# Sorted rows carry their token's number, POOL scatters each tile's results to token order, and batch 0's norm and half its scans move beside tiles

## What is computed

```
expert, layer 0:  silu(x @ wg.T) * (x @ wu.T) @ wd.T           # per token, for its top 2 of 8
scan, layer 1:    s = exp(dt * A) * s + (dt * x) * b           # over 1024 tokens, 16 states a channel
                  y = sum over the states of s * c
expert, layer 1:  square(relu(x @ w_fc.T)) @ w_proj.T          # top 2 of 8, and one shared expert
out:              weight_1 * first choice + weight_2 * second choice + residual, then a norm
```

## Time and profile before

| | |
|---|---|
| median of 3 runs | 1080.74 us (1079.37 to 1081.22) |
| profiled execution | 1075.24 us |
| its span, first to last instruction | 1073.5 us |
| granted TensorE clock, mean | 0.925 of 2.4 GHz |
| busy | PE 913.9, DVE 728.1, ACT 770.0, POOL 501.1 us |
| indirect DMAs | 64 scatters to `xs`, 64 gathers from `ys` |
| stores of tiles by SP | 92 |

### The profile page before, as it was taken

The page is one execution under the profiler, slowest core; times in us unless marked ns, Lnnn a source line. Parts: engine busy times, 40 slices in busy tenths (PEclk is TensorE's granted clock), DMA queues, the critical chain, the costliest instruction groups (busy, mean ns, idle before and its releaser), DMA issues. The chain is left out here.

```text
span 1073.5 us, 34731 instructions
## 1 busy us (share of the span) xinstructions
PE 913.9 (85%) x13676; PEld 858.4 (80%) x13676; DVE 728.1 (68%) x1463; ACT 770.0 (72%) x1275; POOL 501.1 (47%) x385
## 2 busy tenths in 40 slices
PE   4889999999999999999999951899969469899930
PEld 2778998999989989989999841899969359899830
DVE  6699988988998898889888744432459669410202
ACT  5689998988999889989988640544464266598831
POOL 5475755564655555555646116512328152043433
PEclk8799999999999999999999965899999689899975
DMA  8300000000000000000000041313201002023211
GB/s 263 113 2 6 18 3 22 3 3 22 3 3 22 3 22 3 3 23 3 2 22 2 2 177 38 103 54 86 54 26 30 3 28 70 11 68 97 61 55 42
DMA packets 43131, 42.13 MB, mean 39 GB/s; under 512 B 5600, under 2 KB 37344, under 8 KB 42848
## 3 DMA queue, kind: packets, MB, share of 16 engines
q1 hardware_dynamic: 38880, 31.51, 9.6%
q0 software_dynamic: 4096, 8.40, 2.7%
HBM read 25.60 MB, written 14.29 MB: 37 GB/s over the span
## 5 line engine op out<-in xcount | busy, mean ns | idle before, releaser
L557 ACT ACTIVATE Pr<-SC,cur_nesc,cur_esc 128x1024 f32<-128x1024 f32 x256 | 309.9, 1211 | 33.5 <-PE SC L417 17.0
L654 DVE TENSOR_TENSOR Pl<-Pr 128x1024 f16<-128x1024 f32 x224 | 287.5, 1302 | 44.8 <-ACT Pr L557 43.0
L416 PE MATMUL SC<-QK 128*128 128x256 f16 x1024 | 238.7, 274 | 1.0 <-ACT QK L539 1.0
L417 PE MATMUL SC<-QK 128*128 128x256 f16 x1024 | 238.6, 273 | 0.0
L442 PE MATMUL OP<-V,Pr 128*128 128x65 f16 x2048 | 214.4, 192 | 5.8 <-DVE Ob L676 5.7
L444 PE MATMUL OP<-V,Pr 128*128 128x64 f16 x2048 | 215.2, 195 | 0.0
L446 PE MATMUL OP<-V,Pl 128*128 128x65 f16 x2048 | 214.0, 191 | 0.0
L442 PEld LDWEIGHTS OP<-V,Pr 128*128 128x128 bf16 x2048 | 191.0, 97 | 12.5 <-issue 8.2
L444 PEld LDWEIGHTS OP<-V,Pr 128*128 128x128 bf16 x2048 | 190.0, 97 | 2.5
L446 PEld LDWEIGHTS OP<-V,Pl 128*128 128x128 f16 x2048 | 190.7, 99 | 0.0
L789 POOL TENSOR_TENSOR stk<-nrm,stk 128x512 f16<-128x512 f32 x64 | 75.2, 1175 | 147.6 <-DVE stk L636 147.6
(11 more groups left out here) (191 smaller groups left out, 2178.8 us busy)
## 6 DMA issues: line engine op xcount, KB each, us to landing
ys<-yb SPq DMA_DIRECT2D x92, 64.0 KB, 1.5
xg<-xs SPq DMA_DIRECT2D x12, 384.0 KB, 4.4
wst<-in_up SPq DMA_DIRECT2D x8, 512.0 KB, 3.5
xs<-zero SPq DMA_DIRECT2D x2, 1472.0 KB, 13.1
scratch<-in_up SPq DMA_DIRECT2D x1, 2304.0 KB, 8.2
wd<-in_wd SPq DMA_DIRECT2D x4, 576.0 KB, 10.7
wd<-in_wd SPq DMA_DIRECT2D x4, 512.0 KB
QK<-in_wqkv SPq DMA_DIRECT2D x4, 384.0 KB, 7.2
```

The source lines that it names most:

```text
L416: eng.matmul(out, QK[:, b, 1, key:key + P], rhs, start=True, stop=False)
L417: mm = eng.matmul(out, QK[:, b, 2, key:key + P], rhs, start=False, stop=True)
L557: eng.activation(Pr[:, n % PB, :, :], SC[s % 2][:, :, :], ACT.Exp, bias=cur_nesc[:, b:b + 1], scale=cur_esc[:, b:b + 1]).then_inc(s_exps, 1)
L654: eng.tensor_tensor(Pl[:, n % PB, :, :].rearrange("p a b -> p (a b)"), pr, high(pr)[:, 1::2], ALU.subtract).then_inc(s_low_probs, 1)
```

## The change

Each sorted row becomes 528 bytes: behind its 512 bytes stand the number of its token (plus 1024) and its first choice's expert, two numbers of 4 bytes. Slots that no token takes are cleared as before and get a pad: an address past the tokens' rows. As there are now four tensors `xs` and four `ys`, one for each phase, SP clears four in attention, each with a pad's DMA behind it, and waits for them behind the last `wst` load instead of before the first.

When a chunk of sorted rows has been loaded, DVE works out for its rows where the results go (`return_addresses`): first choices to rows 0 to 1023, second choices to 1024 to 2047, pads behind. POOL then writes each tile's results there (`give_back`); SP no longer stores tiles but loads the rows in token order, all four DMAs of a phase after its last tile (`load_rows`). There are 12 buffers `yb` instead of 8.

Batch 0's combination stands at units 28 and 30 (33 and 40 before), its rows at 32 and 33, its turn in two halves at 33 and 34, the convolution at 34, the step products and tanh at 36, the step inputs at 37, and scans 0 to 7 at units 38 to 45, one each, with decays 0 to 9 and state products 0 to 4. From unit 37 on, silu(a) is written as a * (1 + tanh(a / 2)) / 2: ACT makes the tanh, DVE needs two instructions. The other eight scans stay behind the tiles.

On POOL, 7 pieces of `scatter(1)` stand before phase 0's first result and one behind each of its next nine; the pieces of `scatter(3)` stand behind the results of tiles 21 and 22 of phase 2, eight and eight; the power for the norm (2, 1) stands behind the result of tile 2 of phase 2.

Declarations and the constants' small instructions are cut from the diff.

```diff
-        eng.wait_ge(self.s_zero, 1)
-        for b in range(B):
-            eng.dma_start(t["xs"][b].rearrange("(j p) c -> p j c", p=P),
+        eng.wait_ge(self.s_zero, 4)
+        for rows in t["xs"]:
+            rows = rows.rearrange("(j p) c -> p j c", p=P)
+            eng.dma_start(rows[:, :, 0:2 * D],
                           t["zero"][:, :].unsqueeze(1).to_broadcast([P, TILES, 2 * D])).then_inc(self.s_cleared, 16)
-        eng.wait_ge(self.s_loaded, 16 * len(loads))
+            eng.dma_start(rows[:, :, 2 * D:ROW], t["pad"][:, :, :].bitcast(F16)).then_inc(self.s_cleared, 16)
...
+    def sync_ended(self, eng):
+        eng.wait_ge(self.s_loaded, 16 * 9)
         eng.wait_ge(self.s_down, 16 * NC)
-        eng.wait_ge(self.s_cleared, 16 * B)
+        eng.wait_ge(self.s_cleared, 16 * 2 * len(self.t["xs"]))
...
+        eng.iota(self.int_pad[:, :], pattern=[[P, TILES]], base=2 * S, channel_multiplier=1).then_inc(self.s_zero, 1)
+        eng.memset(t["pad"][:, :, 1], -1.0).then_inc(self.s_zero, 1)
+        eng.wait_ge(self.s_zero, 3)
+        eng.tensor_copy(t["pad"][:, :, 0], self.int_pad[:, :]).then_inc(self.s_zero, 1)
...
+            constants.sync_ended(eng)
...
+ROW = 2 * D + 4
...
+FREE_1 = 7
+NORM_3 = 2
+FREE_3 = TILES - 2
+RETURN_2_AT = (9, 10, 11, 12)
+RETURN_AT = (1, 5, 11, 17)
 HR = 3
-YR = 8
+YR = 12
...
-TURN_1 = SHARED_0 - 2
+TURN_1 = 33
+CONVOLVE_0 = TURN_1 + 1
+STEP_0 = TURN_1 + 3
+TANH_0 = STEP_0 + 1
+SCAN_0 = TANH_0 + 1
 STEP_1 = SHARED_0 + 3
 AHEAD = 10
 TURN_2 = SPARSE_2 + 5
+def scans_beside(u):
+    return range(u - SCAN_0, u - SCAN_0 + 1) if u >= SCAN_0 else ()
+def states_beside(u):
+    return range(u - SCAN_0 - 3, u - SCAN_0 - 2) if u >= SCAN_0 + 3 else ()
+def decays_beside(u):
+    if u == TANH_0:
+        return range(0, 2)
+    return range(u - TANH_0 + 1, u - TANH_0 + 2) if u > TANH_0 else ()
...
+        address = split[:, :, :, 2 * D:ROW].bitcast(F32)
+        xg = sb("xg", [P, TILES, ROW], F16)
+        sender = xg[:, :, 2 * D:ROW].bitcast(F32)
...
                 wait(eng, s_sorted_turned, J - TILES + js.stop)
-                rows = xs[ph % 2].rearrange("(j p) c -> p j c", p=P)
+                wait(eng, s_dest, CHUNKS * (ph - 1) + c + 1)
+                rows = xs[ph].rearrange("(j p) c -> p j c", p=P)
                 eng.dma_start(xg[:, js, :], rows[:, js, :]).then_inc(s_sorted_loaded[c], 16)
-            def store(ph, j):
-                J = TILES * ph + j
-                eng.wait_ge(s_down_read, J + 1)
-                eng.dma_start(ys[ph % 2][P * j:P * j + P, :], yb[:, J % YR, :]).then_inc(s_y_stored[J % YR], 16)
+            def load_rows(ph, h):
+                for r in range(YR):
+                    wait(eng, s_y_stored[r], 16 * len(range(r, TILES * ph + TILES, YR)))
+                wait(eng, s_combined, 2 * TB * ph)
+                rows = ys[ph][0:2 * S].rearrange("(k i p) d -> p k i d", k=2, p=P)
+                for k in range(2):
+                    eng.dma_start(yg[:, k, 4 * h:4 * h + 4, :], rows[:, k, 4 * h:4 * h + 4, :]).then_inc(
+                        s_gathered[ph][h], 16)
...
-            for c in range(CHUNKS):
-                load(0, c)
-            for j in range(TILES):
-                store(0, j)
-                if j in (14, 17, 20):
-                    load(1, (j - 14) // 3)
-            load(1, 3)
-            for j in range(TILES):
-                store(1, j)
-            for c in range(CHUNKS):
-                load(2, c)
-            for j in range(TILES):
-                store(2, j)
-            for c in range(CHUNKS):
-                load(3, c)
-            for j in range(TILES):
-                store(3, j)
+            for l in range(2):
+                for b in range(B):
+                    for c in range(CHUNKS):
+                        load(2 * l + b, c)
+                for b in range(B):
+                    for h in range(2):
+                        load_rows(2 * l + b, h)
...
-                if u == TURN_1:
-                    turn(1, 0)
-            step_products(0)
-            for n in range(DS):
+                if u in (TURN_1, TURN_1 + 1):
+                    turn(1, 0, (u - TURN_1,))
+                if u == STEP_0:
+                    step_products(0)
+                if u < SHARED_0:
+                    for n in states_beside(u):
+                        state_products(0, n)
+            for n in range(SHARED_0 - SCAN_0 - 3, DS):
...
+                    if u < TANH_0:
+                        eng.activation(act[:, u % 2, :], AB[u % 2][:, :], ACT.Silu).then_inc(s_activated, 1)
+                    else:
+                        eng.activation(act[:, u % 2, :], AB[u % 2][:, :], ACT.Tanh, scale=0.5).then_inc(s_activated, 1)
...
-                if u == TURN_1 - 2:
-                    rows(1, 0)
-                if u == TURN_1:
-                    read(1, 0)
-            sigmoids(0)
-            for n in range(DS):
+                if u in (TURN_1 - 1, TURN_1):
+                    rows(1, 0, (u - TURN_1 + 1,))
+                if u in (TURN_1, TURN_1 + 1):
+                    read(1, 0, (u - TURN_1,))
+                if u == TANH_0 - 1:
+                    sigmoids(0)
+                if u < SHARED_0:
+                    for n in decays_beside(u):
+                        decays(0, n)
+            for n in range(SHARED_0 - TANH_0 + 1, DS):
...
+                eng.tensor_copy(address[:, b, :, 1], ixf[:, b, 0, :]).then_inc(s_first_choices, 1)
...
+            def return_addresses(ph, c):
+                b, js = ph % 2, chunk_tiles(c)
+                eng.wait_ge(s_sorted_loaded[c], 16 * ph + 16)
+                eng.tensor_tensor(is_first[:, js], sender[:, js, 1], owner[:, b, js], ALU.is_equal).then_inc(
+                    s_is_first, 1)
+                eng.wait_ge(s_is_first, CHUNKS * ph + c + 1)
+                wait(eng, s_y_stored[(TILES * (ph - 1) - 1) % YR],
+                     16 * len(range((TILES * (ph - 1) - 1) % YR, TILES * (ph - 1), YR)) if ph > 1 else 0)
+                eng.scalar_tensor_tensor(out=dest[:, b, js], in0=is_first[:, js], scalar=-float(S),
+                                         in1=sender[:, js, 0], op0=ALU.mult, op1=ALU.add).then_inc(s_dest, 1)
...
-                eng.tensor_tensor(hid[:, u % HR, :], act[:, u % 2, :], UB[u % 2][:, :], ALU.mult).then_inc(s_hidden, 1)
+                h = hid[:, u % HR, :]
+                if u < TANH_0:
+                    eng.tensor_tensor(h, act[:, u % 2, :], UB[u % 2][:, :], ALU.mult).then_inc(s_hidden, 1)
+                    return
+                eng.scalar_tensor_tensor(out=h, in0=act[:, u % 2, :], scalar=1.0, in1=AB[u % 2][:, :], op0=ALU.add,
+                                         op1=ALU.mult).then_inc(s_gated, 1)
+                eng.wait_ge(s_gated, u - TANH_0 + 1)
+                eng.scalar_tensor_tensor(out=h, in0=h, scalar=0.5, in1=UB[u % 2][:, :], op0=ALU.mult,
+                                         op1=ALU.mult).then_inc(s_hidden, 1)
...
-                eng.wait_ge(s_gathered[ph][h], 16 * TB)
+                eng.wait_ge(s_gathered[ph][h], 32)
...
+                if u % TILES in RETURN_AT:
+                    return_addresses(u // TILES, RETURN_AT.index(u % TILES))
+                if u == TURN_1 - 5:
                     combine(0, 0)
                     statistics(1, 0, (0,))
-                if u == 40:
+                if u == TURN_1 - 3:
                     combine(0, 1)
                     statistics(1, 0, (1,))
-                if u == 41:
+                if u == TURN_1 - 2:
                     shifts(1, 0)
-            convolve(0)
-            step_inputs(0)
-            for n in range(DS):
+                if u == CONVOLVE_0:
+                    convolve(0)
+                if u == TANH_0:
+                    step_inputs(0)
+                for n in scans_beside(u):
+                    scan(0, n)
+            for n in range(SHARED_0 - SCAN_0, DS):
...
+                if n in RETURN_2_AT:
+                    return_addresses(2, RETURN_2_AT.index(n))
...
+            for c in range(CHUNKS):
+                return_addresses(3, c)
...
-            def scatter(ph, first=None):
+            def scatter(ph, pieces=range(2 * TB)):
                 b = ph % 2
-                eng.wait_ge(s_slots, ph + 1)
-                eng.wait_ge(s_split_low, ph + 1)
-                for k in range(2):
-                    for i in range(TB):
-                        if first is not None:
-                            wait(eng, s_gate_products, first + TB * k + i)
-                        eng.indirect_dma_start(
-                            out=xs[b], out_offset=bass.IndirectOffsetOnAxis(ap=slots[:, b, k, i:i + 1], axis=0),
-                            in_=split[:, b, i, :], in_offset=None).then_inc(s_scattered[ph], 16)
-            def gather(ph, first=None):
-                b = ph % 2
-                for r in range(YR):
-                    wait(eng, s_y_stored[r], 16 * len(range(r, TILES * ph + TILES, YR)))
```

(54 more changed lines are left out.)

50 lines of the change are left out of this document (29 added, 21 removed).

## The result

The changed kernel took **1088.36 us** (median of 5, 1085.97 to 1093.01), the kernel before 1080.1 beside it: ratio 1.0084, 95% interval 1.0056 to 1.0111. Forecast was 1075.5, faster. The profiled execution took 1088.02 us, its span is 1086.2.

What follows compares the result with a forecast made beforehand. PE sets the tile period, VectorE's scans follow, and PE idles in the tail. Terms -12.0 + 1.0 + 20.1 - 14.3 = -5.2 us put the profiled execution at 1070.0 and the median at 1075.5, range 1063 to 1089.

Steps and rivals of the forecast that it cites:

- Results written by POOL: POOL's scatters replace SP's stores and gathers; POOL keeps up, off PE's path except at waits; together 1.0 us lost.
- Norm and scans: Batch 0's norm and eight scans beside layer 0's tiles, 3.54 us per tile beside a scan: 12.0 us gained.
- choose: One more tiny copy in choose(), 0.1 us, twice on the path: 0.2 us lost.
- Norm (2, 1): Its inverse deviation moves behind the scatter of tile 2; rows and turn end 0.8 us later.
- Late scatter: Last batch's 16 pieces behind tiles 21 and 22: PE stands 17.8 us, half clock costs 2.3; 20.1 us lost.
- Tail: After the last result, scatter then SP loads replace store and gathers: 14.3 us gained (13 to 15.5).
- the span ends 15.0 us behind: Tail term: from the second half's start at 1044.2 to the end at 1059.2, 15.0 us as in the kernel before.
- Start: SP's extra clears and pads during attention: taken at nothing, costing only from 44 ns per pad on.
- rival (c): Pads on SP's queue hold back the first up-weights; at 55 ns per pad the time is 1083.5. Chance 0.1.
- (b): A 528-byte row holds POOL longer than 512: 1085 at 0.3 us more per piece, 1105 if doubled. Chance 0.12.
- (d): Tiles beside scans wait for each other and take 4.5 us: 1083.5. Chance 0.1.
- Rival (a): The late scatter is covered after all, needing 17.8 us from somewhere: time 1055. Chance 0.08.

Runs made afterwards that it cites:

- old_unpaced_again: Second run, in the third sitting, of the kernel before with the pieces of scatter(1) and scatter(3) in a row: 1109.7 us, 1.0291 of before.
- best_rests: Changed kernel with POOL memset pauses, scatter(3) behind tiles 5, 6 and 7, 14 buffers yb, norm (2, 1) power behind tile 0: 1059.25 us, 0.9833 of before.
- after_fourth: The changed kernel, unaltered, in a later sitting without stops: 1070.68 us, 0.9942 of before.
- clears_behind_w0: Changed kernel with SP's eight clearing DMAs behind the first load of up-weights instead of ahead of it: 1071.67 us, 0.9954 of before.
- s3_early_pairs: Changed kernel with scatter(3)'s pieces in pairs behind tiles 6 to 13 of phase 2 instead of 21 and 22: 1054.34 us, 0.9805 of before.
- tail_stored: Changed kernel with the last phase's results stored by SP and gathered by POOL, as before: 1101.4 us, 1.0216 of before.
- after: The changed kernel's first measurement and its profile: 1088.36 us, 1.0084 of before.
- early_pairs_rests: s3_early_pairs plus a POOL memset behind each piece of scatter(1) and scatter(3) and each result of phases 0 and 2: 1061.42 us, 0.9839 of before.
- half rests: early_pairs_rests with the memset at 256 columns instead of 512: 1058.44 us (0.9834 of before), again 1056.9 us (0.9818).
- third sitting: Set run together (a sitting): changed kernel 1083.36 us, s3_early_pairs 1085.98, old_unpaced_again 1109.7, early_pairs_rests 1061.42.
- old_unpaced: First run of the kernel before with the pieces of scatter(1) and scatter(3) in a row: 1075.69 us, 1.0006 of before.

## Why the prediction was wrong, and where it was right

**The step that failed** is in "Results written by POOL": "it keeps up ... No DMA of POOL is then on the path of PE". I asked only whether POOL has the time (2.5 us against 2.4) and who waits for its DMAs. POOL did keep up; the loss was that PE stops, and ACT and DVE behind it, while POOL issues without a pause. The two kinds of sitting differ in tile 0 to 34 by 9.3 us (93.6 against 84.3), in tile 60 to 69 by 3.7, in tile 46 to 60 by 0.8. The kernel before doesn't show it: its scatter and gather pieces beside tiles are held to one per tile, and its unbroken stretches stand where PE waits anyway. That this is the reason old_unpaced_again shows, which lifts the holding and took 1109.7 us in a sitting where the kernel before took 1078.8. Nothing in the trace of before priced an unbroken stretch beside running engines. The sign came out wrong in three of four measurements of the changed kernel (1.0084, 1.004, 1.0043) and right in the fourth (0.9942, against 0.9952 for -5.2 us). How near the fourth comes is in part luck: by its trace the sum is -3.6, of terms that miss by up to 3.4 us, some one way and some the other.

**Norm and scans: right, 2 us too good.** Forecast -12.0 and 0.2 for choose; the table shows -9.8 and -9.7, undoing it 10.6 to 11.9. The period was right to 0.03 us; missing were DVE's waits of 2.2 and 0.5 us behind the last tile. **Norm (2, 1)**: 0.8 forecast; tile 46 to 60 took 0.6 to 1.3 us more than before in the eight traces without stops, and no more where the power stands behind tile 0 (best_rests).

**Late scatter: right in size.** 20.1 forecast, 19.2 in after_fourth, and 0.9 more in the tiles behind it; over both stages the five traces with the late scatter and no stops give 19.9 to 20.6. The wait is 18.5 to 18.7 us in them where 17.8 was said (the sum as written gives 17.7), and the slow tiles behind it, at a granted clock of 0.50 to 0.62 until 996 us in after_fourth, cost 1.4 to 2.0 us and not 2.3. But where there are stops its place is no mistake: spread early, it saved 19.8 us without stops (tile 60 to 69: 50.9 in clears_behind_w0, 31.1 in s3_early_pairs) and nothing with them (1085.98 against 1083.36).

**Tail: mis-sized.** -14.3 forecast, -17.6 measured, -17.5 by undoing it. From the last result's read to the second half's sum it takes 10.3 us (1064.92 to 1075.23) where I had 9.6: the scatter starts 0.8 late and SP spends 0.8 on its twelve waits, against 0.6 won on loads and sums. The term that failed is "the span ends 15.0 us behind", copied from the kernel before: it is 11.0 now. The last rows on ScalarE start 7.4 us before the end (1078.78), before 11.4, with the same instructions behind them; what the span of the kernel before has there for 4 us, no row of either trace names, and tail_stored has it again (11.2).

**Start: taken at nothing, but not free.** Tile 0 is read 0.2 to 5.2 us later than in the trace of before, 2.4 on average, in the 14 traces with the eight clears in the changed place. Three things can be told apart.
- The longer row, which I had not priced on this path: from the first piece of scatter(0) to the first turn it takes 25.1 to 25.4 us in the three traces of the old rows and 25.8 to 26.4 in all 17 of the new. Most of it is the first load of sorted rows, which lands 3.7 to 4.3 us after its issue where the old one took 3.27 and 3.41.
- The first weights, my rival (c). A write of 8 bytes took 25 to 31 ns on average, over the 13 to 24 that I took and under the 44 from which on it costs. But the last was written at 70 to 77 us, not between 53 and 61, and SP, which spent 6.5 to 7.5 us on the issue of each of these DMAs but the first (after), got to the first weights at 62 to 68. In 3 of the 14 traces ScalarE waited for them, by 0.9 to 1.8 us.
- That is not all: with the first weights ahead of the clears ScalarE read them no earlier (80.99 and 81.56), and with the clears later attention lost more. The first piece of scatter(0) came at 651.1 us on average over the 14 and at 649.0, 649.8 and 651.1 in the old order; the ranges overlap, so that this 1.1 us is not clear of the spread. What the eight clears disturb in attention stays open.

**Rivals (b) and (d) were false**: a scatter of 528 bytes holds POOL 0.96 us, a tile beside a scan takes 3.51. Rival (a) was false too: without stops the wait was there in full.

**Still open**: what in the machine stops PE; what makes a sitting one kind or the other (one and the same chip had a sitting of each kind); and how long a pause is enough: 0.54 us of memset was, in one program and one sitting, and 0.33 was never tried where there are stops. The traces have a mark that goes with the sitting and not with the order: the records of semaphores raised by DMAs. Kernels whose results POOL writes leave 2698 to 3054 of them in sittings with stops and 3488 to 3749 in the others, though they issue the same DMAs (but for the last phase of tail_stored). early_pairs_rests, which has no stops, has 2737, so that it did run where the others stop. Why records are missing no run shows, nor whether the recording has a part in the stops.

Of the versions here, early_pairs_rests is the only one shown faster than both kernels where there are stops (0.9839). Without stops early pairs alone has the lowest ratio (0.9805), with the half rests inside its interval (0.9818 and 0.9834).

## What to carry to other kernels

Beside running engines, leave a pause between POOL's indirect DMAs, or hold them to one per tile; an unbroken row of them stopped PE in mid-stream in three of six sittings, and ACT and DVE behind it, even though nobody waited for the data. When a gap's releaser is "issue" or "remote", look at what POOL does at that moment. A pause has its price too: it delays what POOL writes, and with it the rows and the buffers that others wait for. And run the unaltered kernel again beside the experiments: four experiments in a sitting without stops would have led me to a wrong account if I had compared them with the first measurement.

## What the runs showed that I had not expected

- A sitting can hold a whole set of kernels at a level of its own: the same program took 1054.34 and 1085.98 us, another 1075.69 and 1109.7, while the kernel before moved by 2.4 us (1076.4 and 1078.8).
- In the third sitting 16 indirect DMAs in a row (20.2 us) left PE 7.4 busy us of 24.
- The stops look like engines that wait for instructions, but they did not end with the arrival of any. In after no packet of the queues called "instruction" is recorded from 978 to 1011 us, while ACT, DVE and PE go on at 1004.13, 1004.22 and 1004.66. In old_unpaced_again there is none from 681.2 to 698.6, while DVE, ACT and PE go on at 691.49, 693.52 and 693.96, and none from 963 to 987, while ACT and PE go on at 982.54 and 983.01. What they went on with had arrived before. Beside running engines such packets come every 8 us or so: three of queue q8 in old_unpaced from 941 to 963 (packets, MB, share):

```profile
q8 instruction: 3, 0.05, 1.0%
```
